# Where a projection's bias is added: to the rows of x on VectorE in the first stage, instead of by products in the second

## The reference, cut to what matters

```python
x = L0_attn_x                                  # (2, 4096, 512), float32
mod = silu(c) @ wmod                           # six rows of 512 for each of two batches
sa, ca, ga, sb, cb, gb = mod                   # ga and gb are held at 0.25 or more in size
h = layernorm(x) * (1 + ca) + sa
q, k, v = split(h @ w_qkv.T)                   # relu(q), relu(k); 16 heads of 32
vk = v_with_a_row_of_ones @ k.T                # per head, over all 4096 rows of a batch
out = (vk @ q)[:-1] / (vk @ q)[-1]
x = x + ga * (out @ w_proj.T + b_proj)         # the change is about ga * b_proj
h = layernorm(x) * (1 + cb) + sb
x = x + gb * experts(h)                        # 8 experts, the two best for each row
```

## Time and profile before

| | |
|---|---|
| median of 3 runs | 2190.42 us (2183.8 to 2192.34) |
| profiled execution | 2185.83 us, span 2183.8 us |
| busy over the span: TensorE, VectorE, ScalarE, GpSimd | 95%, 61%, 36%, 37% |
| mean granted TensorE clock | 0.977 |
| first stage | until about 600 us |
| second stage | about 600 to 985 us |
| third stage | the rest |

### The profile page before, as it was taken

How to read it: one execution, slowest core, us unless ns; L and a number is a source line. 1 busy time by engine, 2 the same in 40 slices (tenths; PEclk the granted TensorE clock), 3 DMA queues, 4 the chain that set the end, 5 groups by cost and what they waited for, 6 DMA issues and landing times.

```text
span 2183.8 us, 42589 instructions
## 1 busy us (share of the span) xinstructions
PE 2069.7 (95%) x9416; PEld 1620.3 (74%) x9417; DVE 1330.8 (61%) x3179; ACT 792.1 (36%) x1493; POOL 804.5 (37%) x622
## 2 busy tenths in 40 slices
PE   7999999999979999974999999999999999999997
PEld 5888878888846666653788888887878778888885
DVE  7555554555368888873556556555555456565654
ACT  3444434444346666651222222222222232222222
POOL 5676756566415666751111111111111111121111
PEclk9999999999989999996999999999999999999998
DMA  8766565656545676776855558558765975865543
GB/s 275 253 201 207 169 206 169 207 168 207 184 143 204 234 266 221 268 273 203 218 128 126 129 137 233 126 129 238 197 171 127 288 176 127 232 137 127 127 107 77
DMA packets 293833, 404.89 MB, mean 185 GB/s; under 512 B 50648, under 2 KB 188888, under 8 KB 285920
## 3 DMA queue, kind: packets, MB, share of 16 engines
q1 hardware_dynamic: 166304, 259.74, 37.7%
q0 software_dynamic: 30096, 72.12, 15.7%
q10 hardware_dynamic: 97200, 70.82, 10.4%
HBM read 210.57 MB, written 191.98 MB: 184 GB/s over the span
## 4 chain that ended last, share of the span: by engine, by line
PE 46%; DMA 4%; SPq 2%; issue 1%; ACTq 1%; DVE 0%; ACT 0%; POOL 0%; DVEq 0%
PE bank L1755 46%; DMA act_rows<-hact 2%; DMA wbuf<-expert_split 1%; SPq L561 1%; ACTq L1042 1%; DMA expert_rows<-rows,dest 0%; SPq L563 0%; SPq L559 0%; DVE act_t_lo L1635 0%; SPq L534 0%; DVE orow L1663 0%; DMA arow<-act_rows 0%; SPq L567 0%; SPq L568 0%; POOL expert_rows L752 0%
## 5 line engine op out<-in xcount | busy, mean ns | idle before, releaser
L1755 PE MATMUL bank<-wbuf,x_t_hi 128*128 x2160 | 684.0, 398 | 34.6 <-DVE x_t_lo L1618 30.9
L773 POOL DMA_INDIRECT out_rows<-orow,cur_tok x135 | 209.0, 1548 | 973.5 <-DVE orow L1663 775.4
L1755 PEld LDWEIGHTS bank<-wbuf,x_t_hi 128*128 128x128 f32 x2160 | 409.5, 190 | 133.9 <-issue 36.8
L1755 PE MATMUL bank<-wbuf,x_t_lo 128*128 x1080 | 428.9, 397 | 0.0
L1755 PE MATMUL bank<-wbuf,act_t_hi 128*128 x1080 | 343.4, 399 | 11.2 <-DVE act_t_lo L1635 10.0
L1624 DVE TENSOR_TENSOR hact<-bank,gact 128x512 f32<-128x512 f32 x135 | 93.2, 690 | 377.1 <-PE bank L1755 374.1
L1755 PEld LDWEIGHTS bank<-wbuf,act_t_hi 128*128 128x128 f32 x1080 | 204.8, 190 | 63.5 <-issue 15.3
L1755 PEld LDWEIGHTS bank<-wbuf,x_t_lo 128*128 128x128 f32 x1080 | 205.1, 190 | 48.8
L1755 PE MATMUL bank<-wbuf,act_t_lo 128*128 x540 | 214.8, 398 | 0.0
L1024 ACT ACTIVATE x_t_hi<-bank 128x512 fp32r<-128x512 f32 x135 | 81.0, 600 | 297.5 <-PE bank L1755 286.9
L1048 ACT ACTIVATE act_t_hi<-bank 128x512 fp32r<-128x512 f32 x135 | 80.9, 599 | 296.5 <-DMA arow<-act_rows 201.6
(11 more groups left out here) (225 smaller groups left out, 3869.3 us busy)
## 6 DMA issues: line engine op xcount, KB each, us to landing
wbuf<-expert_split SPq DMA_DIRECT2D x24, 1536.0 KB, 9.5
xrow<-expert_rows SPq DMA_DIRECT2D x540, 64.0 KB, 3.2
act_rows<-hact ACTq DMA_DIRECT2D x135, 256.0 KB
arow<-act_rows ACTq DMA_DIRECT2D x540, 64.0 KB
expert_split<-split_hi SPq DMA_DIRECT2D x32, 768.0 KB, 3.4
expert_split<-split_lo SPq DMA_DIRECT2D x32, 768.0 KB, 5.9
q_rows<-qf SPq DMA_DIRECT2D x16, 1024.0 KB, 6.7
qb<-q_rows SPq DMA_DIRECT2D x16, 1024.0 KB, 11.0
```

Of the source, the lines that this page charges most:

```text
L773: pool.indirect_dma_start(out=out, out_offset=bass.IndirectOffsetOnAxis(cur_tok[at][:, 0:1], 0), in_=orow[at % 2][:, :], in_offset=None, c ...
L1755: last = mm(dst, stationary(a, f), moving(b, f), start=(first and k == 0), stop=(k == parts * n - 1))
```

## The change

A new DRAM tensor `x_bias_rows` takes x plus ga times b_proj. In the first stage x is loaded once more, into a single new buffer `xe` of one group; VectorE adds `gab` to its four tiles, SyncE stores it, and the second stage loads its residual rows from there. The products with `bias_r`, and what prepares them, are gone. Two small constants (`item_no`, `padrow`) move to the second stage's memory, and `silu_c` shares the new buffer, which makes room. `gab` exists only after group 2, so 16 sets are spread over groups 3 to 15: one for each group, two for 7, 8 and 13 (`again_in`).

```diff
+    def again_in(g, b):
+        if not isinstance(g, int):
+            return (g - 3,) if b == 0 else (g - 1,)
+        if g < 3:
+            return ()
+        if g <= GPB:
+            return (2 * g - 10, 2 * g - 9)
+        return (NG - 4, NG - 3) if g == NG - 3 else (g,)
...
     def phase1_over(eng):
...
+        eng.wait_ge(s_xes, 16 * NG)
...
+        def load_again(e):
+            wait_apart(sp, s_xes, 16 * e)
+            sp.dma_start(xe[:, :, :], group_rows(x, e)).then_inc(s_xe, 16)
+        def store_bias(e):
+            sp.wait_ge(s_xea, TPG * (e + 1))
+            sp.dma_start(group_rows(xd, e), xe[:, :, :]).then_inc(s_xes, 16)
...
             if has(g, 2):
                 load_x1(g + 2)
+            for e in again[:1]:
+                store_bias(e)
+            for e in again[1:]:
+                load_again(e)
             if not last:
                 store_expert(g, 1)
                 load_expert_raw(g + 1, 1, 1 - par)
+            for e in again[1:]:
+                store_bias(e)
+            if isinstance(g, int) and g == 2:
+                sp.dma_start(xe[:, :, :], group_rows(x, 0)).then_inc(s_xe, 16)
+            elif again and not last:
+                load_again(again[-1] + 1)
             wait_apart(sp, s_qst, 16 * g)
...
         def load_x(g, par):
             wait_apart(sp, s_x2, 16 * g)
-            sp.dma_start(xb[par][:, :, :], group_rows(x, g)).then_inc(s_x2, 16)
+            sp.dma_start(xb[par][:, :, :], group_rows(xd, g)).then_inc(s_x2, 16)
...
-        act.activation(part_r[:, :], ones_f[:, :], ACT.Copy, scale=2.0 / P).then_inc(s_bias, 1)
-        act.activation(bias_r[:, :, :], gab[:, :, :], ACT.Copy).then_inc(s_bias, 1)
...
+        def add_bias(e, b):
+            dve.wait_ge(s_xe, 16 * (e + 1))
+            dve.wait_ge(s_gab, B)
+            for t in range(TPG):
+                tt(xe[:, t, :], xe[:, t, :], gab[:, b, :], ALU.add).then_inc(s_xea, 1)
...
             ts(ve[:, :], mv[:, :, 1], LN_EPS, None, ALU.add).then_inc(s_var, 1)
+            for e in again[:1]:
+                add_bias(e, b)
             dve.wait_ge(s_seed, g + 1)
             newton(lns, y0[:, :], ve[:, :], nt1[:, :], nt2[:, :])
...
                 if t == TPG - 1:
                     add_zk(g)
+                    for e in again[1:]:
+                        add_bias(e, b_again)
...
-        tt(bias_r[P // 2:, :, :], gab[P // 2:, :, :], f32(bias_r[P // 2:, :, :]), ALU.subtract).then_inc(s_bias, 1)
...
-            mm(dst, part_r[:, :], bias_r[:, b, :], start=True, stop=False)
```

More of the change, by code:

```diff
@@ L116, in build @@
     mod_d = nc.dram_tensor("mod_rows", (B, 4 * C), F32, kind="Internal").ap()
+    xd = nc.dram_tensor("x_bias_rows", (NT, C), F32, kind="Internal").ap()
     xs = nc.dram_tensor("expert_rows", (E * CAP + P, ROW), F32, kind="Internal").ap()
@@ L137, in build @@
     lane = sb(keep, "lane", [P, 1], F32)
-    item_no = sb(keep, "item_no", [P, ITEMS], F32)
     modcol = sb(keep, "modcol", [P, 2 * FC * B], F32)
@@ L153, in build @@
     add_f = sb(keep, "add_f", [P, E], F32)
-    padrow = sb(keep, "padrow", [P, ROW], F32)
     pad_to = sb(keep, "pad_to", [P, E], U32)
@@ L174, in build @@
     qf = [sb(ph1, f"qf{i}", [P, FC, GT], F32) for i in range(2)]
+    xe = sb(ph1, "xe", [P, TPG, C], F32)
     sa_ks = qf[0]
@@ L182, in build @@
     c_exp = sb(ph1, "c_exp", [P, FC * B], F32)
-    silu_c = sb(ph1, "silu_c", [P, FC, NBLK * 8], F32)
+    silu_c = xe[:, 0:FC, 0:NBLK * 8]
     st = sb(ph1, "st", [P, TPG, 6], F32)
@@ L205, in build @@
     ln_eps = sb(ph2, "ln_eps", [P, 1], F32)
-    part_r = sb(ph2, "part_r", [P, P], F32R)
-    bias_r = sb(ph2, "bias_r", [P, B, C], F32R)
     less_sel = sb(ph2, "less_sel", [P, P], F32)
@@ L234, in build @@
     ntli = sb(ph2, "ntli", [P, E], I32)
+    padrow = sb(ph2, "padrow", [P, ROW], F32)
+    item_no = sb(ph2, "item_no", [P, ITEMS], F32)
     it_e, it_r, it_t, it_k = (sb(ph2, f"it_{i}", [P, ITEMS], F32) for i in range(4))
@@ L280, in build @@
     s_gab = sem("gab_ready")
+    s_xe, s_xea, s_xes = sem("x_again_loaded"), sem("x_bias_added"), sem("x_bias_stored")
     s_hi, s_lo, s_elo = sem("split_hi"), sem("qkv_split_lo"), sem("expert_split_lo")
@@ L464, in _ @@
         sp.dma_start(pes_bc[:, :], pes.partition_broadcast(P)).then_inc(s_const, 16)
+        def load_again(e):
[4 more added lines that the diff above has]
+            sp.dma_start(group_rows(xd, e), xe[:, :, :]).then_inc(s_xes, 16)
         def group1(g, par, b):
             last = not has(g, 1)
+            again = again_in(g, b)
             store_expert(g, 0)
@@ L721, in _ @@
         pool.memset(padrow[:, :], 0.0).then_inc(s_padi, 1)
+        pool.iota(item_no[:, :], [[1, ITEMS]], base=0, channel_multiplier=0, allow_small_or_imprecise_dtypes=True).then_inc(s_free, 1)
         pool.wait_ge(s_padi, 1)
@@ L1098, in _, with stats1 @@
         lns = Steps(dve, s_ln, 2 * TPG + 3)
-        def stats1(g):
+        def add_bias(e, b):
[3 more added lines that the diff above has]
+                tt(xe[:, t, :], xe[:, t, :], gab[:, b, :], ALU.add).then_inc(s_xea, 1)
+        def stats1(g, again=(), b=0):
             lns.begin(g)
@@ L1226, in group1 @@
             if ends_batch(g):
-                dve.wait_ge(s_id, 16)
+                dve.wait_ge(s_id, 15)
                 keep_ksums(0, ZK_B[1])
@@ L1232, in group1 @@
                 kq_lo(3)
+            again = again_in(g, b)
+            b_again = 0 if ends_batch(g) else b
             if more:
-                stats1(g + 1)
+                stats1(g + 1, again, b_again)
+            elif again:
+                add_bias(again[0], b_again)
             if isinstance(g, int) and g == 0:
@@ L1825, in group1 @@
             if ends_batch(g):
-                pe.wait_ge(s_id, 16)
+                pe.wait_ge(s_id, 15)
                 pe.wait_ge(s_zka, GPB)
@@ L1911, in project @@
             at_least(pe, s_x1, TPG * g + t - 1)
-            if g == 0 and t == 0:
-                pe.wait_ge(s_bias, 3)
-            mm(dst, part_r[:, :], bias_r[:, b, :], start=True, stop=False)
             if t == 0:
@@ L1917, in project @@
             product(dst, 3, FC, lambda a, f: on[par][a][:, f, t * P:(t + 1) * P],
-                    lambda k, f: kvp[k][:, b, f, :], first=False, between=between).then_inc(s_y, 1)
+                    lambda k, f: kvp[k][:, b, f, :], between=between).then_inc(s_y, 1)
         def turn_h2(g, par, t):
```

6 lines of the change are left out of this document (2 added, 4 removed).

## The result

The changed kernel takes 2346.77 us (median of 4 runs, 2338.57 to 2352.87), the kernel before 2190.47 us (4 runs) on the same chip: a ratio of 1.0704, 95% interval 1.0682 to 1.0726. It is slower, as forecast, but by 156 us and not by 109, which puts it 12 us above the range.

A forecast was written before the change was run, and what follows sets the result against it. Bound: saturated TensorE with 0.14 us slack in the first stage, VectorE's order and scatters in the second. 57.6 + 5 + 34.2 + 15.2 = 112 us, less 3, is 109 on the median: 2299 us, range 2250 to 2335.

The forecast's parts named there:

- 7.2 us of TensorE's time in a group: First stage, single groups: newton starts 19.7 instead of 12.4 us after the fourth transposition, stopping TensorE 7.2 us (bounds 4.8, 9.5).
- The landing: First stage: the load of xe lands at T (end of a group's fourth transposition) + 17.2 us, bounds 14.8 and 19.5.
- The clock: Rival, first stage: same stall plus clock dips on the path at twelve longer stalls, 20 us more, 2319 us; chance 0.09.
- The groups with two sets: First stage, groups 7, 8 and 13: two sets through one buffer; 17.1 us each in 8 and 13, 15.2 in 7.
- beside the 17: Double groups: TensorE's next k product starts 13 us later, parallel to the 17 us stall, so not added.
- the 21 us: Second stage: 64 removed bias products at 0.33 us each, the upper bound of the gain if all stood on the path.
- The -3: Second stage: removed products save 3 us, from 12 projections in the first two groups and the last.
- Smaller stall: Rival: the bias store hides entirely and the second stage returns all 21 us, giving 2252 us; chance 0.12.
- Faster: Rival: load lands by 9.9 us after the fourth transposition, additions vanish, 21 us of products come off, 2169 us; chance 0.04.
- no change: Rival: the load is in time and the removed products were off the path, 2187 us; chance 0.03.
- In time, but blocked: Rival: rows in time, but additions beside GpSimd's k_lo and k_sum take 6.2 us, 34 us slower, 2225 us; chance 0.03.
- the additions themselves cost nothing: First stage, VectorE: four additions, 2.5 us, fit the 3.6 us gap before the seed if rows are there in time.

The follow-up runs named there:

- the filler products: Changed kernel plus 26 unused products on TensorE ahead of its wait for k_lo, in the loops' 8 groups: 2333.61 us, 1.0626 of the kernel before.
- the additions alone: Changed kernel's first stage, with its loads, additions and stores, then the second stage of the kernel before, bias products included: 2342.96 us, 2338.01 us when run again.

## Why the prediction was right, and where it failed

**What bounds the kernel** was read rightly: a saturated TensorE with 0.14 us of slack behind newton, z and GpSimd's fixed order. Undoing only the place of the wait (the additions behind z) removes all but 0.4 us of the loss of a single group.

**The order of events** was right in each step: a load held behind the bias store, splits and raw, VectorE idle 8.65 us (some 8 forecast), then newton, k_lo, the zk product, no relief from group to group.

**The step that failed is the price of a group, "7.2 us of TensorE's time in a group".** It measured 9.3 to 9.9 us, once 11.5. Two terms of it were mis-sized: the store ahead of the load, taken at 2.4 us, delayed it by about 4, and the clock, taken at nothing in the sum, cost 2.0. The terms, for the group shown:
- The landing, taken at T + 17.2 us with 19.5 as the upper bound: T + 19.5, 2.3 us more. The forecast was the landing of the store of q in the same place, T + 14.8, plus 2.4 us for the bias store ahead. That store measured 4.3 us, read on the loads of raw behind it, and the run without it puts them back where they were; that is 1.9 us of the miss. It had been priced at the best rate seen, with a part of it fitted into a stretch with a free share; nothing of it was hidden. The other 0.4 us is the load itself, 2.6 us behind the last raw, where the store of q took 2.2.
- The clock, +2.0 us (14.7 less 12.7), confirmed by the filler products. The prediction had it as a rival with a chance of 0.09 and 1.7 us for each dip: right in size for a dip, wrong in likelihood. Over the whole stage it is 32 us of busy time and not the 20 of that rival, as the waits of the double groups and of group 7 have their dips too. Its counter-argument, that a dip just after T lies in new slack, doesn't apply: the dip lies at the end of the wait, on the path to T.
- Newton without GpSimd beside it, -1.6 us (8.54 less 10.17), not foreseen. It hides a part of the two misses: TensorE's wait for k_lo, 6.6 us, looks like the "some 7 us" of the forecast by this chance. With it the terms give 7.2 + 2.3 + 2.0 - 1.6 = 9.9 us, the 45.0 of this group.

**The groups with two sets** were given 17.1 us over before and took 22.6 and 23.0; the same mis-sized term, repeated. Each 1 MB transfer took 6.7 to 8.8 us, so the second additions began at T + 32.5 us instead of 27. **Group 7** took 20.3 us instead of 15.2, for the same reason: its zk product starts at T + 38.7 us and not at T + 34.4 (389.88, with T at 351.2). The k product that was forecast to run "beside the 17" at T + 18.6 came at T + 21.1.

**The second stage** was forecast 3 us shorter; it came out 5.7 us longer than in the kernel before, and equal (410.9 and 410.3) beside the kernel that keeps the products. VectorE's waits from 770 to 1132 us:
```profile
DVE rows L1389 <- DMA expert_rows<-rows,dest: 15.4, 17, 4.1
DVE x L1344 <- PE bank L1796: 15.0, 13, 4.0
```
It waits for the scatters 15.4 us, where it was 21.3 in the same part of the kernel before (618 to 975 us), and for projections 15.0 us where it was 10.3: shorter projections did not shorten its waits. That most of the 21 us is hidden was right. The -3 is below what could be resolved, and so are most of the 5.7 us: two profiled executions of the same kernel differ by 3.9 us here (414.8 and 410.9 with the change, 414.2 and 410.3 for the additions alone). Over all profiles the stage takes 409.1 to 414.2 us with the 64 products and 410.6 to 416.7 with none. What moves it is open.

**The third stage's** +4.6 us: it varies from 1169.7 to 1182.5 us between kernels with identical code and data for it, so it is not put down to the change.

**The rivals.** *Smaller stall*: the bias store didn't hide. *Faster* and *no change*: excluded by the load (their bound, that nothing of 1 MB landed under 4.5 us after issue, has one exception before, a store of q at 594.7 us with 3.9 us; it changes nothing). *In time, but blocked*: by the run with gab in place of x the blocking exists and costs 13 us between the medians, not 34; four additions took 4.7 us and not the 6.2 assumed. Of "the additions themselves cost nothing" only this is left: it holds when they come late, while GpSimd is idle.

**The sum with the measured terms**: 78.7 + 5.8 + 45.6 + 20.3 + 1.3 = 151.7 us in the first stage, of 156 us between the medians. Of the 40 us that the forecast lacked there, 21 are in the single groups, 11 in groups 8 and 13, 5 in group 7.

## What to carry to other kernels

When one engine is saturated, ask for each in-order engine that feeds it how late its next result may be; a load placed in an idle gap is free only if it has landed when the gap opens, and with the same work one place later in the program (behind z instead of before newton) the loss fell from 7.0% to 3.1%. In these full queues a transfer's landing followed what was issued ahead of it and not what came behind, so price an added transfer by how much later everything behind it lands (3.8 to 4.3 us for this store of 1 MB), and not by its size over the best rate seen (2.6 us). And a wait of 6.6 us that repeats in each group cost 2 us more than its length here, as the clock fell in it and the first products after it paid.

## What the runs showed of the hardware

- In a wait of TensorE of 6.6 us the granted clock went from 1.00 to 0.50 and stood there from some 200.5 to 207.4 us, 4.3 us of it under products that then took 0.43 us each instead of 0.23. With 26 unused products in place of the wait it stayed at 1.00.
- Four additions of 128x512 with both operands in SBUF take 2.50 us with GpSimd idle, 4.68 us beside k_lo and k_sum, and 6.53 us in the place behind z.
- DMA engines at a full share moved anything from 230 to 436 GB/s in stretches of 2 us of such a mix of stores and loads.
- A store of 1 MB issued ahead made the transfers behind it land 3.8 to 4.3 us later.
- A load of 1 MB took 9.6 us to land with a 1 MB store issued right behind it and 9.6 us without.
